# A post-norm decoder layer in f32: cross attention without a query projection, with keys projected by a product of both weights

## What is computed

```python
def _L0_xattn_ref(queries, keys, values, Wq, bq, Wk, bk, Wv, bv):
    Q = jnp.einsum('bsd,ed->bse', queries, Wq) + bq
    K = jnp.einsum('bsd,ed->bse', keys, Wk) + bk
    V = jnp.einsum('bsd,ed->bse', values, Wv) + bv
    scores = jax.nn.relu(jnp.einsum('bqd,bkd->bqk', Q, K))
    return jnp.einsum('bqk,bkd->bqd', scores, V)
...
x = _layernorm(x + _L0_xattn_ref(x, ctx_1024, ctx_1024, ...), axis=-1)
```

## Time and profile before

| | us |
|---|---|
| median of 3 runs | 199.77 |
| lowest and highest | 198.17, 200.55 |
| the profiled execution | 199.57 |
| its span, first to last instruction | 197.7 |

### The profile page before, as it was taken

How to read it: one execution, slowest core, us unless ns; L and a number is a source line. 1 busy time by engine, 2 the same in 40 slices (tenths; PEclk the granted TensorE clock), 3 DMA queues, 4 the chain that set the end, 5 groups by cost and what they waited for, 6 DMA issues and landing times. The chain is left out here.

```text
span 197.7 us, 3675 instructions
## 1 busy us (share of the span) xinstructions
PE 145.5 (74%) x1156; PEld 105.1 (53%) x1166; DVE 126.5 (64%) x327; ACT 68.7 (35%) x154; POOL 49.3 (25%) x57
## 2 busy tenths in 40 slices
PE   2899655859963898659966599399649779999800
PEld 1466433546642685446745357256434269899800
DVE  6657968799698757989476863333237005888850
ACT  3310016332262722553225721211200058677500
POOL 7459900400003001030040304110314000253562
PEclk9999988699997899996999969859997999999995
DMA  4765648469901360000000000000650665740000
GB/s 124 200 186 189 192 136 231 127 202 239 333 22 45 88 217 12 0 0 0 5 31 0 0 3 14 14 0 3 184 172 27 185 201 168 217 136 26 12 26 23
DMA packets 17734, 19.72 MB, mean 100 GB/s; under 512 B 2607, under 2 KB 13364, under 8 KB 17282
## 3 DMA queue, kind: packets, MB, share of 16 engines
q1 hardware_dynamic: 15898, 17.28, 29.8%
q0 software_dynamic: 752, 1.21, 2.5%
q10 hardware_dynamic: 1064, 0.98, 1.7%
HBM read 14.48 MB, written 5.18 MB: 99 GB/s over the span
## 5 line engine op out<-in xcount | busy, mean ns | idle before, releaser
L933 DVE TENSOR_REDUCE mx<-ps_s 128x4 f32<-128x1024 f32 (+1 forms) x24 | 28.4, 1219 | 5.0 <-PE ps_s L719 5.0
L953 DVE SCALAR_TENSOR_TENSOR es<-es,tab_sb 128x1024 f32<-128x1024 f32 x24 | 28.4, 1220 | 5.1 <-ACT es L601 5.1
L601 ACT ACTIVATE es<-ps_s 128x1024 f32<-128x1024 f32 x24 | 23.7, 1024 | 15.2 <-PE ps_s L741 15.1
L513 POOL TENSOR_TENSOR rstd<-var,mhalf 128x2 f32<-128x2 f32 x8 | 8.2, 1024 | 65.1 <-DVE var L891 65.0
L527 POOL DMA_INDIRECT out<-qx x13 | 12.8, 984 | 29.1 <-issue 21.0
L719 PE MATMUL ps_s<-kx,qx 128*128 128x256 bf16 (+1 forms) x128 | 18.3, 258 | 1.8 <-issue 0.8
L741 PE MATMUL ps_s<-qx,kx 128*128 128x128 bf16 (+1 forms) x128 | 16.9, 278 | 1.4 <-ACT es L601 0.8
L521 POOL DMA_INDIRECT sorted_dram<-x,slot x8 | 8.1, 1011 | 32.4 <-DVE slot L1019 31.2
L715 PE MATMUL ps_s<-maskb,identb 128*128 128x256 bf16 (+1 forms) x41 | 12.9, 314 | 3.9 <-DVE mx L933 3.6
L862 PE MATMUL ps_m<-w_sb,es 128*128 x104 | 14.8, 285 | 1.1 <-ACT es L654 0.8
L654 ACT ACTIVATE es<-ps_s,b_sb 128x128 f32<-128x128 f32 x52 | 14.8, 367 | 1.8 <-PE ps_s L854 0.8
(11 more groups left out here) (127 smaller groups left out, 235.7 us busy)
## 6 DMA issues: line engine op xcount, KB each, us to landing
es<-w1T SPq DMA_DIRECT2D x13, 256.0 KB, 3.0
w_sb<-w2T SPq DMA_DIRECT2D x8, 256.0 KB, 5.8
qx<-q_dram SPq DMA_DIRECT2D x9, 192.0 KB
kx<-k_dram SPq DMA_DIRECT2D x9, 192.0 KB
sorted_dram<-blank SPq DMA_DIRECT2D x8, 198.0 KB
q_dram<-parts SPq DMA_DIRECT2D x20, 64.0 KB, 2.1
ctxT_sb<-ctxT SPq DMA_DIRECT2D x2, 512.0 KB, 5.5
qx<-sorted_dram SPq DMA_DIRECT2D x13, 66.0 KB, 2.6
```

What stands on the lines that cost most here:

```text
L601: act.activation(es[:, k % EBUF, :], sc[:, :], ACT.Exp, scale=float(DK) ** -0.5).then_inc(free, 1)
L933: ins = v.tensor_reduce(mx[:, b % 2, h0:h0 + n, t], sc[:, :].rearrange("p (h k) -> p h k", h=n), AX.X, ALU.max)
L953: v.scalar_tensor_tensor(out=e, in0=e, scalar=CEIL, in1=decay[:, 0:qs].unsqueeze(1).to_broadcast([P, nh, qs]), op0=ALU.min, op1=ALU.mult). ...
```

## The change

The cross scores are (x1 Wq' + bq)(c Wk' + bk)', with c a context row. They are regrouped as x1 (c M + Wq' bk)' + c (Wk' bq) + bq bk, with M a product of both weights. So nothing is projected on the query side: keys are made by M, with a column added, and what comes from the query bias is one number per key (`beta`), which is the bias of the relu, where keys lie on the partitions.

- START: a new piece `weave` (both weights transposed on PE, copied by DVE to `pair`, and two small DVE instructions) between proj(0) and proj(1), and `fold` (M and three columns: four products on PE, copied by DVE) after proj(1). `ctx` now uses `fold` and waits for it.
- EARLY is 2: START holds ctx 0 and 1, FIRST ctx 2, and round 1 ctx 3, between cross(0) and the second shift.
- New pieces `beta`: four products of one moving column each, and an addition on DVE; beta(0) at the end of FIRST, and beta(r) in round r, after relu.
- `q2` is gone, on PE and on ACT. In the rounds relu now stands directly after ("max", 1, 3), ahead of ("pv", 0, 0); in CHAIN it follows x1t, and rank(2) comes after relu. Two `warm` pieces (2 and 1 matmuls) are gone.
- The relu on ACT is four ACTIVATEs of 256 columns with a bias each; the first two wait only for half of the scores.

```diff
-EARLY = 3
-START = [("proj", 0, 0), ("proj", 1, 0), ("rouse", 0, 0), ("ctx", 0, 0), ("ctx", 1, 0), ("ctx", 2, 0),
+EARLY = 2
+START = [("proj", 0, 0), ("weave", 0, 0), ("proj", 1, 0), ("fold", 0, 0), ("rouse", 0, 0), ("ctx", 0, 0), ("ctx", 1, 0),
          ("max", 0, 0), ("max", 0, 1), ("max", 0, 2),
          ("max", 0, 3), ("shift", 0, 0), ("max", 0, 4), ("max", 0, 5), ("shift", 0, 1)]
 FIRST = [("exp", 0, 0), ("exp", 0, 1), ("exp", 0, 2), ("proj", 2, 0), ("max", 1, 0), ("exp", 0, 3), ("max", 1, 1),
          ("exp", 0, 4), ("max", 1, 2), ("exp", 0, 5), ("pv", 0, 0), ("max", 1, 3), ("pv", 0, 1), ("shift", 1, 0),
-         ("max", 1, 4), ("max", 1, 5), ("ctx", 3, 0), ("shift", 1, 1)]
+         ("max", 1, 4), ("max", 1, 5), ("ctx", 2, 0), ("shift", 1, 1), ("beta", 0, 0)]
 ROUND = [("pv", -1, 2), ("max", 1, 0), ("pv", -1, 3), ("evac", -1, 0), ("max", 1, 1), ("x2t", -2, 0),
          ("max", 1, 2), ("turn", -1, 0), ("exp", 0, 0), ("exp", 0, 1), ("back", -1, 0), ("out", -1, 0),
          ("exp", 0, 2), ("norm1", -1, 0), ("proj", 2, 0), ("route", -2, 0), ("exp", 0, 3), ("exp", 0, 4),
-         ("x1t", -1, 0), ("exp", 0, 5), ("max", 1, 3), ("q2", -1, 0), ("pv", 0, 0), ("relu", -1, 0),
+         ("x1t", -1, 0), ("exp", 0, 5), ("max", 1, 3), ("relu", -1, 0), ("beta", 0, 0), ("pv", 0, 0),
          ("pv", 0, 1), ("rank", -2, 0), ("shift", 1, 0), ("max", 1, 4), ("max", 1, 5), ("cross", -1, 0),
-         ("shift", 1, 1), ("norm2", -1, 0)]
+         ("ctx", 2, 0), ("shift", 1, 1), ("norm2", -1, 0)]
 CHAIN = [("pv", -1, 2), ("pv", -1, 3), ("evac", -1, 0), ("turn", -1, 0), ("back", -1, 0), ("out", -1, 0),
          ("x2t", -2, 0), ("warm", -1, 8), ("norm1", -1, 0), ("route", -2, 0), ("x1t", -1, 0),
-         ("warm", -1, 2), ("q2", -1, 0), ("rank", -2, 0), ("warm", -1, 1), ("relu", -1, 0), ("cross", -1, 0),
+         ("relu", -1, 0), ("rank", -2, 0), ("cross", -1, 0),
          ("warm", -1, 6), ("norm2", -1, 0), ("x2t", -1, 0), ("warm", -1, 2), ("route", -1, 0),
          ("rank", -1, 0), ("warm", -1, 18)]
...
-        q2T = sb("q2T", [P, S])
+        pair = sb("pair", [P, 2, D])
+        both = sb("both", [P, 1])
+        ones32 = sb("ones32", [P, 1])
+        fold = sb("fold", [P, D + 3])
+        beta = sb("beta", [P, B, KT])
...
                 if kind == "ctx" and b >= EARLY:
+                    taken(act, "m", ("fold", 0, 0))
                     k2, free = filled(act, "m", piece, 0)
-                    act.activation(k2T[:, b, :], k2[:, :], ACT.Identity, bias=cols_sb[:, XBK:XBK + 1])\
+                    act.activation(k2T[:, b, :], k2[:, :], ACT.Identity, bias=fold[:, D:D + 1])\
                         .then_inc(free, 1)
...
-                if kind == "q2":
-                    at, free = filled(act, "m", piece)
-                    act.activation(q2T[:, :], at[:, 0:S], ACT.Identity, bias=cols_sb[:, XBQ:XBQ + 1]).then_inc(free, 1)
                 if kind == "relu":
-                    at, free = filled(act, "s", piece)
-                    act.activation(sc2[:, :, :], at[:, :].rearrange("p (k q) -> p k q", k=KT), ACT.Relu)\
-                        .then_inc(free, 1)
+                    slot, _n = place[(*piece, 0)]
+                    at = ps_s[slot]
+                    taken(act, "m", ("beta", b, 0))
+                    act.wait_ge(relu_half, b + 1)
+                    for k in range(KT):
+                        if k == KT // 2:
+                            at, free = filled(act, "s", piece)
+                        ins = act.activation(sc2[:, k, :], at[:, k * S:(k + 1) * S], ACT.Relu, bias=beta[:, b, k:k + 1])
+                    ins.then_inc(free, 1)
                 if kind == "x2t":
...
-                    pe.matmul(k2[:, :], W(XK), cT, start=True, stop=True).then_inc(full, 1)
+                    taken(pe, "m", ("fold", 0, 0))
+                    pe.matmul(k2[:, :], fold[:, 0:D], cT, start=True, stop=True).then_inc(full, 1)
                     v, full = vacant(pe, "m", piece, 1)
...
-                if kind == "q2":
+                if kind == "weave":
+                    pe.wait_ge(ld_w, 16)
+                    pe.wait_ge(consts, 1)
+                    at, full = vacant(pe, "m", piece)
+                    for i, w in enumerate((XQ, XK)):
+                        mm = pe.transpose(at[:, i * D:(i + 1) * D], W(w), ident[:, :])
+                    mm.then_inc(full, 1)
+                if kind == "fold":
+                    taken(pe, "m", ("weave", 0, 0))
+                    pe.wait_ge(fold_cols, 2)
+                    at, full = vacant(pe, "m", piece)
+                    pe.matmul(at[:, 0:D], pair[:, 1, :], pair[:, 0, :], start=True, stop=True)
+                    pe.matmul(at[:, D:D + 1], pair[:, 0, :], cols_sb[:, XBK:XBK + 1], start=True, stop=True)
+                    pe.matmul(at[:, D + 1:D + 2], pair[:, 1, :], cols_sb[:, XBQ:XBQ + 1], start=True, stop=True)
+                    pe.matmul(at[:, D + 2:D + 3], ones32[:, :].to_broadcast([P, P]), both[:, :], start=True, stop=True).then_inc(full, 1)
+                if kind == "beta":
+                    cT = ctxT_sb[:, b * SK:(b + 1) * SK]
+                    at, full = vacant(pe, "m", piece)
+                    for t in range(KT):
+                        mm = pe.matmul(at[:, t:t + 1], cT[:, t * P:(t + 1) * P], fold[:, D + 1:D + 2], start=True, stop=True)
+                    mm.then_inc(full, 1)
+                if kind == "relu":
                     taken(pe, "m", ("x1t", b, 0))
-                    at, full = vacant(pe, "m", piece)
-                    pe.matmul(at[:, 0:S], W(XQ), x1T[:, :], start=True, stop=True).then_inc(full, 1)
-                if kind == "relu":
-                    taken(pe, "m", ("q2", b, 0))
                     taken(pe, "m", ("ctx", b, 0))
                     at, full = vacant(pe, "s", piece)
                     for k in range(KT):
-                        mm = pe.matmul(at[:, k * S:(k + 1) * S], k2T[:, b, k * P:(k + 1) * P], q2T[:, :],
+                        mm = pe.matmul(at[:, k * S:(k + 1) * S], k2T[:, b, k * P:(k + 1) * P], x1T[:, :],
                                        start=True, stop=True)
+                        if k == KT // 2 - 1:
+                            mm.then_inc(relu_half, 1)
                     mm.then_inc(full, 1)
...
+                if kind == "weave":
+                    nat, free = filled(v, "m", piece)
+                    v.tensor_copy(pair[:, :, :], nat[:, 0:2 * D].rearrange("p (i d) -> p i d", i=2)).then_inc(free, 1)
+                    v.memset(ones32[:, :], 1.0).then_inc(fold_cols, 1)
+                    v.tensor_tensor(both[:, :], cols_sb[:, XBQ:XBQ + 1], cols_sb[:, XBK:XBK + 1], ALU.mult).then_inc(fold_cols, 1)
+                if kind == "fold":
+                    g, free = filled(v, "m", piece)
+                    v.tensor_copy(fold[:, :], g[:, 0:D + 3]).then_inc(free, 1)
+                if kind == "beta":
+                    bt, free = filled(v, "m", piece)
+                    taken(v, "m", ("fold", 0, 0))
+                    v.tensor_scalar(beta[:, b, :], bt[:, 0:KT], fold[:, D + 2:D + 3], None, ALU.add).then_inc(free, 1)
+                    taken(v, "m", piece)
                 if kind == "ctx":
                     if b < EARLY:
-                        v.wait_ge(ld_cols, 16)
+                        taken(v, "m", ("fold", 0, 0))
                         k2, free = filled(v, "m", piece, 0)
-                        v.tensor_scalar(k2T[:, b, :], k2[:, :], cols_sb[:, XBK:XBK + 1], None, ALU.add).then_inc(free, 1)
+                        v.tensor_scalar(k2T[:, b, :], k2[:, :], fold[:, D:D + 1], None, ALU.add).then_inc(free, 1)
```

4 lines of the change are left out of this document (3 added, 1 removed).

## The result

The kernel became slower: 205.60 us median of four executions (203.59 to 206.93) against 200.03 for the kernel before on the same chip, a ratio of 1.026 (95% interval 1.015 to 1.037). In a second, later comparison of the same two kernels it was 1.037 (1.031 to 1.042). The profiled span grew from 197.7 to 203.9 us. Some executions of a program fall into a slower state; the ratios and their intervals leave these out, the medians hold all. I had forecast 201.3, and 203.2 as the upper end.

The account below looks back on a forecast made before the run. No engine alone bounds the kernel: PE and DVE alternate in the rounds, a relay forms the last chain, DMA and DVE the start. -0.5 + 1.4 + 1.7 + 0.5 - 1.7 = +1.4, rounded to +1.5: 201.3 us, range 198.3 to 203.2.

Parts of the forecast that it names:

- The chain, -1.7: Last chain, batch 3's x1t to cross: q2 and its copy gone, relu shorter; 1.7 us gained.
- POOL's tie with the second scatter: Last chain: POOL free of the later second scatter just as var of cross(3) comes, at 141.4; at most 0.1 us lost.
- beta(0), +1.4: End of FIRST: PE waits for a PSUM buffer, then beta takes 0.85 us; DVE idle, so 1.4 us lost.
- the 0.2 us that I took off for the last pass's latency: Pricing of beta's eight passes: some 0.2 us subtracted for the last pass's latency, giving 0.85 us.
- Round 1, +1.7: Round 1: beta against q2 and relu's place cost 0.6 us, ctx(3) 1.1; bounds 0.6 to 2.6.
- Rounds 2 and 3, +0.5: Rounds 2 and 3: beta against q2 costs 0.27 us each, 0.5 together; no ctx there.
- The start, -0.5: START: one ctx less lets PE reach the maximum scores some 1 us earlier; DVE gains 0.5 us at most.
- rival C: Start: proj(1) and ctx(0) wait longer, +1.5 us instead of -0.5; total 202.5 to 203.5 us; chance 0.14.
- FIRST, 0: From DVE's first maximum to its second shift of batch 1, most of FIRST: no change forecast, 0 us.
- The queues behind `rank(2)`: Tail: blanks about 1.2 us later hold POOL's last scatters till 149.4 to 150.2; gain should survive, with no slack left.
- Rival D: Tail: blanking and scatters end 1.2 us later, tokens load only 0.5 us earlier; +2.6, 202.4 us; chance 0.14.

Follow-up runs that it names:

- the second trace: The changed kernel, unaltered, profiled again in the second comparison with the kernel before: 205.6 us against 198.15, ratio 1.037.
- the kernel before with one more POOL addition: Kernel before plus a POOL addition of the residual's shape into an unread buffer, beside batch 2's parts: 200.75 us against 197.11.
- two queues: Changed kernel with four of the eight blanking DMAs after rank(2) issued by ACT instead of SP: 203.62 us, ratio 1.028.
- `rank(2)` first: Changed kernel with rank(2) back ahead of the relu in CHAIN, where it stood before the change: 202.60 us, ratio 1.023.
- three ctx: Changed kernel with EARLY = 3: three ctx in START, the fourth in FIRST, none in round 1: 208.07 us, ratio 1.042.
- `rank(2)` late: Kernel before with only rank(2) moved behind the relu's score matmuls of batch 3: 201.58 us against 199.49.
- beta later: Changed kernel with each beta one round later, before the relu using it, and six warm matmuls instead of eight in CHAIN: 206.08 us, ratio 1.033.
- the residual late: Changed kernel with POOL's residual addition waiting until DVE has written batch 2's parts: 205.31 us, ratio 1.042.
- The versions that also mend FIRST: Changed kernel with rank(2) ahead of relu and residual addition delayed: 205.6 us; also all betas later: 205.0; or only beta(0) in round 1: 202.98.

## Why the prediction was wrong, step by step

- **The chain, -1.7: right.** From x1T's copy to z of cross(3) it was 5.45 us (138.40 to 143.85, and 5.45 in the second trace) instead of 7.12 before (7.11 in the kernel before with one more POOL addition), 1.67 less. POOL's tie with the second scatter was one: rstd started at 145.43, with no idle time before it.
- **beta(0), +1.4: right**, measured 1.56. The group of eight passes took 1.05 us (0.95 in the rounds) rather than 0.85: no run shows the 0.2 us that I took off for the last pass's latency.
- **Round 1, +1.7: right in sum** (1.57 and 1.98). The part of ctx(3), forecast at 1.1, is shown: 1.07 in both traces and gone when ctx(3) is moved back. The part of beta and the relu's place (forecast 0.6, measured 0.5 and 0.9) isn't clear of the scatter.
- **Rounds 2 and 3, +0.5: not resolved.** -1.33 in one trace, +0.39 in the other of the same program, and the kernel before itself took 40.05 and 38.32 us in two traces. One thing that differs in both pairs is POOL's power in round 2: it took 0.69 us in the kernel after and in the kernel before with one more addition, and 1.54 in the kernel before and in the second trace of the kernel after, where DVE's multiplication of two SBUF tensors had started 0.24 us ahead of it. DVE then waits for that power.
- **The start, -0.5: wrong, by too small a price for the half clock.** Its own terms (ctx(0) 2.1 us later, one ctx less 2.1) leave PE no earlier; the "some 1 us earlier" and with it "DVE can gain the time between, 0.5 us" need PE back at full clock for the second ctx. Start of the kernel after, which answers the earlier trace rows:

```profile
14.01 2.04 PE L705 MATMUL ps_m<-ctxT_sb,fold 128*128 128x512 f32 x2 [0.48 <-DVE fold L958]
...
15.84 1.91 PE L708 MATMUL ps_m<-w_sb,ctxT_sb 128*128 128x128 f32 x8
...
17.55 1.54 PE L705 MATMUL ps_m<-ctxT_sb,fold 128*128 128x512 f32 x2
...
19.82 0.38 PE L726 MATMUL ps_s<-maskb,identb 128*128 128x512 bf16 x1
...
20.90 3.49 DVE L976 TENSOR_REDUCE mx<-ps_s 128x8 f32<-128x1024 f32 x3 [0.19 <-PE ps_s L730]
```

  The eight passes on values took 1.91 us, against 1.05 at full clock, and PE came to the first scores at 19.82, 0.9 us later than before. In the second trace the same group started at 14.15 and took 1.05; PE was done with both ctx at 17.42 instead of 18.83 and then waited 1.35 us for `kx<-k_dram`: there the operands' arrival capped the gain, at 0.13. This is part of rival C, about 1 us of it.
- **FIRST, 0: wrong, a term that I hadn't looked for.** I followed what reads DVE's results but not what else runs beside DVE. Before, the parts of batch 2 are over just when POOL's addition starts; these rows of the trace of before would have shown it:

```profile
35.78 0.42 DVE L920 TENSOR_TENSOR parts<-rest,parts 128x256 bf16<-128x256 f32 x1
...
36.21 2.34 POOL L507 TENSOR_TENSOR x_sb<-x_sb,rows_sb 128x1024 f32<-128x1024 f32 x1 [10.94 <-issue]
```

  One microsecond later on DVE, with the addition tied to a DMA's arrival, they collide. Timeline of the kernel after:

```profile
36.13 2.35 POOL L513 TENSOR_TENSOR x_sb<-x_sb,rows_sb 128x1024 f32<-128x1024 f32 x1 [10.74 <-issue]
...
35.35 0.29 DVE L948 CAST parts<-rest 128x256 bf16<-128x256 f32 x1
...
36.53 2.09 DVE L948 CAST parts<-rest 128x256 bf16<-128x256 f32 x1
```

  A delay of 0.9 us at the start cost 1.8 more. The kernels with two queues, with `rank(2)` first and with three ctx, whose start was late as well (20.94 to 23.55), also have one long cast or subtraction (1.93 to 2.47 us). In the second trace FIRST lost 2.77 in another way: the start was on time and no cast was long, but SP's issue of two k stores took 2.53 us at 24.18, against 1.24 before at 23.88, and the loads of batch 1 were issued late. Whether that issue is the cause, and what made it long, no run tests.
- **The queues behind `rank(2)`: the step that failed, and it holds most of the error.** The prediction had the mechanism: "the blanks hold them till 149.4 and some start-up, 149.4 to 150.2", with "no slack left". Taken relative to x1T the blanks' main traffic did end there (153.2 - 3.84 = 149.4). Three sizes were wrong. First, from the end of the traffic to the scatter's start there are about 1.4 us (149.7 to 151.12 in the kernel before with `rank(2)` late), which I had put at 0 to 0.8. Second, in all five traces of the changed chain with the eight blanks on SP (both of the kernel after, and those with beta later, three ctx and the residual late) a thin remainder ran on for some 1.3 to 1.6 us behind the main traffic. DMA engines' busy tenths and GB/s of the kernel after, 150 to 154 us in 40 slices, and 154 to 158:

```profile
DMA  0069999972000499998830002899999400000000
GB/s 0 5 201 317 317 296 306 290 233 64 0 0 0 127 275 285 301 444 280 248 101 5 0 0 63 243 306 317 306 312 270 116 11 16 21 21 21 16 16 16
...
GB/s 21 16 16 16 16 0 0 0 0 0 0 0 0 0 0 0 0 0 0 0 0 123 246 184 287 307 348 287 225 266 226 307 225 246 184 225 310 289 225 248
```

  The tenths show 0 from 153.2 on, but 11 to 21 GB/s still flow until 154.5, and the scatter starts 1.4 us behind that. The mean share of 16 engines rounds so little to nothing. In the trace of before no such remainder ran on, so the earlier trace rows didn't hide it, and with `rank(2)` alone moved in the kernel before there is none either. GB/s there, 147 to 153 us:

```profile
GB/s 292 275 67 0 4 232 306 306 303 190 11 0 77 299 306 299 282 88 0 0 0 0 0 0 0 0 0 0 0 0 0 0 0 0 0 0 0 0 137 191
```

  So it is hardly chance, and what makes it the runs don't show. Together these put the scatters at 152.05 relative to before instead of 149.4 to 150.2. Third, I let the token load start when the last scatter's traffic ends (3.1 us behind the first of the last scatters); in the kernel after that traffic ended at 159.0 to 159.3 and the load was issued at 160.32, 4.43 us behind that scatter. The three add up: 1.3 for the remainder, 0.6 for the blanks' landing beyond the 0.8 allowed, and 1.3 for that of the scatter are the 3.2 us by which the load is late.

The Trainium skill, page "DMA: Bandwidth & Descriptors", section "Anatomy of one DMA — SWDGE (gpsimd) path", puts most of a DMA's fixed 2 us into the receipt that the last byte has landed, after which the semaphore rises. That section is on DMAs that GpSimd issues, as the scatters here are: 1.0 to 1.3 us passed between their last traffic and the token load that waited for them. The 1.4 us behind the blanks, which SP issues, are of the same kind. I should have priced both waits so.

Rival D was thus the right one by its mechanism, given too small a chance (0.14) and too small a price: 202.4 for a gain that shrinks, whereas the gain turned into a loss of 1.5 and a colder start of the experts. The sum fits: the forecast's 1.4, plus 1.4 for the start, 1.8 for FIRST, 3.2 for the token load and 0.9 for the experts, less 1.8 in the rounds and 0.95 of the one long stretch in the trace of before, gives 6.0 of 6.2 measured. The last two, 2.8 us, are luck: stretches in which traces of one program differ. Without it the trace would have been further from the forecast.

What stays open: whether the change can be made to win. With `rank(2)` first, one edit, it loses 2.3% instead of 3.7. The versions that also mend FIRST gained there what their traces show, and took 2 to 4 us more in the last chain than the one with `rank(2)` first alone (13.80 to 15.32 against 11.48), with PE at its lower clock, in all three that were tried. None was as fast as the kernel before.
